# Writing GpSimd's indexed fetches of a four-layer graph network out tile by tile

## The reference

```
x = x + L0(relu(layernorm(x)))   # 4-head attention: q[src]*k[dst], softmax over each dst, sum of v[src], gate, layernorm
x = x + L1(relu(layernorm(x)))   # edge weight = sigmoid(mlp(x[src], x[dst])), symmetric degree norm, sum of (x W)[src]
x = x + L2(relu(layernorm(x)))   # two graph convolutions in a row, each a normed sum of (x W)[src] over dst
x = x + L3(relu(layernorm(x)))   # 4-head graph attention: leaky(e_l[src]+e_r[dst])+log(w), softmax, sum of (x W)[src]
```

## Time and profile before

| | us |
|---|---|
| median of three runs | 8741.41 |
| lowest and highest | 8729.65, 8745.29 |
| span of the profiled execution | 8272.4 |

### The profile page before, as it was taken

One profiled execution on the slowest core, in us unless ns is written; L12 is line 12 of the kernel. 1 busy time (PEld: TensorE's weight loads), 2 busy tenths in 40 slices (PEclk: granted clock), 3 DMA queues, 4 the chain that ended last, 5 costly groups with the idle time before them and its releaser, 6 DMA issues. The chain is left out here.

```text
span 8272.4 us, 99941 instructions
## 1 busy us (share of the span) xinstructions
PE 3960.1 (48%) x22250; PEld 3653.4 (44%) x22250; DVE 3397.9 (41%) x8039; ACT 2027.6 (25%) x3881; POOL 4970.2 (60%) x5007
## 2 busy tenths in 40 slices
PE   4444442553666665666333333433333545454166
PEld 3444441552666665566333333433333444444155
DVE  4333336776444444776322222322222311111586
ACT  1000000773333333996000000000000200000176
POOL 3777772541777775332577777477777277777254
PEclk8555555986666666877656555755555655555599
DMA  5666662441555554663111111111111244444154
GB/s 159 183 180 182 182 182 81 142 121 47 136 134 133 135 137 125 193 196 123 42 47 47 47 47 46 42 47 47 47 47 48 48 96 99 99 99 96 42 155 120
DMA packets 973113, 863.79 MB, mean 104 GB/s; under 512 B 350004, under 2 KB 837256, under 8 KB 972808
## 3 DMA queue, kind: packets, MB, share of 16 engines
q1 hardware_dynamic: 798344, 452.32, 19.6%
q0 software_dynamic: 159744, 356.39, 16.9%
q10 hardware_dynamic: 14976, 54.53, 2.0%
HBM read 669.20 MB, written 193.56 MB: 104 GB/s over the span
## 5 line engine op out<-in xcount | busy, mean ns | idle before, releaser
L768 POOL DMA_INDIRECT sum_rows<-tab_row,sum_idx x1664 | 1644.5, 988 | 631.5 <-issue 470.9
L905 DVE TENSOR_TENSOR acc<-acc,sum_pA 128x128 f32 x4160 | 984.8, 288 | 1846.0 <-PE sum_pA L802 1766.4
L391 PE MATMUL l_pK<-l_winr,l_hotT 128*128 128x128 f32 (+2 forms) x4992 | 1128.0, 399 | 1044.1 <-ACT l_hotT L433 396.2
L391 PEld LDWEIGHTS l_pK<-l_winr,l_hotT 128*128 128x128 f32 x4992 | 1075.7, 327 | 1139.9 <-issue 600.0
L802 PE MATMUL sum_pA<-sum_hot,sum_rows 128*128 128x128 f32 x3328 | 772.8, 426 | 1596.7 <-DMA sum_rows<-tab_row,sum_idx 1596.7
L802 PEld LDWEIGHTS sum_pA<-sum_hot,sum_rows 128*128 128x128 f32 x3328 | 719.7, 328 | 1649.7 <-DMA sum_rows<-tab_row,sum_idx 867.7
L373 POOL DMA_INDIRECT l_rows<-tab_ax,l_idx x832 | 878.1, 1055 | 316.4 <-issue 235.4
L373 POOL DMA_INDIRECT l_rows<-tab_qv,l_idx x832 | 861.9, 1036 | 316.4 <-issue 220.8
L373 POOL DMA_INDIRECT l_rows<-tab_wh,l_idx x832 | 808.2, 971 | 316.3 <-issue 230.9
L802 PE MATMUL sum_pA<-sum_hot,sum_wrow 128*128 128x128 f32 x4992 | 738.8, 310 | 416.5 <-DVE sum_hot L261 233.2
L802 PEld LDWEIGHTS sum_pA<-sum_hot,sum_wrow 128*128 128x128 f32 x4992 | 679.1, 219 | 464.7 <-POOL sum_wrow L737 272.4
(11 more groups left out here) (233 smaller groups left out, 4482.7 us busy)
## 6 DMA issues: line engine op xcount, KB each, us to landing
spill<-l_rows SPq DMA_DIRECT2D x312, 512.0 KB, 3.4
sum_rows<-spill SPq DMA_DIRECT2D x312, 512.0 KB
l_winr<-tab_k SPq DMA_DIRECT2D x840, 64.0 KB
sum_line<-src_lo ACTq DMA_DIRECT2D x104, 512.0 KB, 4.5
l_winr<-tab_b SPq DMA_DIRECT2D x840, 32.0 KB
sum_rows<-tab_row,sum_idx POOLq DMA_INDIRECT x1664
l_winr<-tab_er SPq DMA_DIRECT2D x840, 2.0 KB
l_rows<-tab_qv,l_idx POOLq DMA_INDIRECT x832
```

Of the source, the lines that this page charges most:

```text
L391: last = nc.tensor.matmul(pK[:, b, u, :], hotT[:, b, u, :], winr[:, b * TB + u, :], start=True, stop=True)
L768: nc.gpsimd.indirect_dma_start(rows[:, u, :], None, tab_row, bass.IndirectOffsetOnAxis(idx[:, u:u + 1], 0)).then_inc(s_rows[b], 16)
L905: nc.vector.tensor_tensor(acc[:, u % 2, bass.ds(at, P)], acc[:, u % 2, bass.ds(at, P)], pA[:, b, u, :], ALU.add).then_inc(s_add, 1)
```

## The change

In both functions GpSimd's hardware loop is replaced by a Python loop over all 104 batches, so the 832 indirect DMAs of a phase stand in the code one after the other, and each reads its indices from its own column of `src_idx`. The tile `idx`, the copy, the semaphore `s_idx` and its two waits are gone. The waits for a free half and for the spill keep their counts, now constants. The loops of all other engines stay.

```diff
-                        with pool.Fori(0, ROUNDS) as i:
-                            for b in range(2):
-                                pool.wait_ge(s_used, i * 2 + b + 1)
-                                pool.wait_ge(s_spill[b], i * 16 + 16)
-                                nc.gpsimd.tensor_copy(idx[:, b * TB:(b + 1) * TB],
-                                                      src_idx[:, bass.ds((i * 2 + b) * TB, TB)]).then_inc(s_idx, 1)
-                                pool.wait_ge(s_idx, 1)
-                                pool.wait_ge(s_idx, i * 2 + b + 1)
-                                for u in range(b * TB, (b + 1) * TB):
-                                    nc.gpsimd.indirect_dma_start(
-                                        rows[:, u, :], None, table,
-                                        bass.IndirectOffsetOnAxis(idx[:, u:u + 1], 0)).then_inc(s_rows[b], 16)
+                        for n in range(BATCHES):
+                            b = n % 2
+                            pool.wait_ge(s_used, n + 1)
+                            pool.wait_ge(s_spill[b], 16 * (n // 2) + 16)
+                            for u in range(TB):
+                                t = n * TB + u
+                                nc.gpsimd.indirect_dma_start(
+                                    rows[:, b * TB + u, :], None, table,
+                                    bass.IndirectOffsetOnAxis(src_idx[:, t:t + 1], 0)).then_inc(s_rows[b], 16)
```

23 lines of the change are left out of this document (8 added, 15 removed).

## The result

| | before | after |
|---|---|---|
| median (20 runs each, in turns), us | 8744.34 | 8763.37 |
| lowest, highest | 8727.09, 8770.09 | 8741.39, 8783.59 |
| profiled execution, own time | not given | 8780.58 |
| its span | 8272.4 | 8778.8 |

After over before is 1.0018, with a 95% interval of 1.001 to 1.0025. The change makes the kernel 19 us slower, and the forecast was 377 us less.

What follows compares the result with a forecast made beforehand. GpSimd's own stream was taken to bound the five fetch phases. Boundaries save 352 us and collisions 25, together 377, so 8741.4 falls to 8364 us; the forecast's own range is 8320 to 8412, with two rivals 8250 to 8520.

Steps and rivals of the forecast that it cites:

- The removed part: GpSimd's batch boundaries in five phases: without copy, semaphore and loop, gaps fall from 0.975 to 0.305 us, 352 us saved.
- The collisions: GpSimd fetches starting under VectorE instructions with two SBUF inputs: cost falls from 244 to 219 us, a gain of 25.
- the replay: Last 103 batches of each phase recomputed with fetches at their new places: 17, 59, 34, 36 and 73 us of collisions.
- The rule of 0.82: A fetch starting under a VectorE instruction with two SBUF inputs ends no earlier than 0.82 us behind that instruction.
- all on the path, since GpSimd waits for nobody: All five phases last as long as GpSimd's own stream, so the whole 352 us saved at boundaries shortens the kernel.
- over 4 us of cover: Used rows, needed free about 10.2 us behind a batch's last fetch, are free by about 5.6 to 5.8 us.
- I keep the 469 as it is: The runs' median lies 469 us above the profiled span; this unexplained part was taken to stay constant.
- One of the prediction's own signs of being wrong: Idle of GpSimd before fetches put down to VectorE, TensorE or the spill would show the forecast wrong.
- GpSimd's pace being set by something unseen: Rival: the change doesn't do what it says and the time stays the same; chance 0.03.
- The score passes are held by transfers: Rival: SyncE's windows or the DMA engines become the bound, only the sums gain, 133 us: 8608 us; chance 0.04.
- the second rival: More is gained: collisions vanish with small shifts, or the 469 us is a stretch; 8250 to 8315 us, chance 0.08.
- The slower rival: GpSimd's 4160 unrolled fetches wait for instruction blocks; at 10 us for each of 49 blocks 8854 us; chance 0.07.

Runs made afterwards that it cites:

- x_before: The kernel before, run and recorded again unchanged; 8649.83 us, 1.0017 of the kernel before.
- a_pace_score: The changed kernel with a 1,024-column memset and a wait for it ahead of each batch in the three score passes only; 8453.32 us, 0.9788 of the kernel before.
- a_fetchonly: The changed kernel with sums 2 and 3 reduced to their fetches, VectorE running a free loop in sum 3; 8788.39 us, 1.0175 of the kernel before.
- a_fo_rate: The changed kernel, both sums only fetches with VectorE's free loop, rests of 1,024 columns (sum 2) and 1,536 (sum 3); 8814.24 us against 8654.08 for before.
- a_pace1024: The changed kernel with a 1,024-column memset and a wait for it ahead of each batch, in all phases; 8503.15 us, 0.9879 of the kernel before.
- a_pace2048: The changed kernel with a 2,048-column memset and a wait for it ahead of each batch, a rest of 2.09 us; 8756.58 us, 1.013 of the kernel before.
- a_half: The changed kernel with each fetch of the two plain sums cut from 128 to 64 rows, the others zeros; 8700.0 us, 1.01 of the kernel before.

## Why the prediction was wrong

**The removed part was right.** The gap at a boundary is 0.305, the fetch's median 0.944 to 0.946 (0.947 to 0.949 before), and GpSimd's first fetch starts at 117.9, 2.2 us earlier. If the stops are taken out, GpSimd's own stream (busy time, gaps inside batches, 0.305 at 103 boundaries) is 1083, 1100, 1109, 1115 and 1093 us, together 5500. The forecast's five phases sum to 5504.

**The collisions were right in sum.** They cost 29, 52, 64, 69 and 43 us (busy time less 832 medians), 257 where the replay had 219. The sums have more and score 3 less than forecast; the replay knew of no stops, and these shift the fetches against VectorE. The rule of 0.82 held: the fetch of 4567.82 starts under the one-hot that ends at 4568.31 and ends at 4569.13.

```profile
4566.57 0.94 POOL L756 DMA_INDIRECT sum_rows<-tab_row,src_idx  x1 [0.30 <-issue]
4567.09 1.22 DVE L261 TENSOR_TENSOR sum_hot<-iota,local 128x1024 f32<-128x1024 f32 x1
4567.82 1.31 POOL L756 DMA_INDIRECT sum_rows<-tab_row,src_idx  x1 [0.30 <-issue]
```

The one-hot starts inside the fetch of 4566.57, which keeps its 0.94. So this trace differs again from the Trainium skill, "SBUF — State Buffer", section "SBUF: two separate sides", by which the first of the two holds the port pair for its whole instruction.

**The step that failed is "all on the path, since GpSimd waits for nobody", with its "over 4 us of cover".** The phases took 6394 us and not 5504: 890 us of stops, 713 of them in the score passes and 179 in the sums. The cover was computed with VectorE's and SyncE's instructions at the speed that they had in the recording. That speed didn't hold: single register instructions took 0.70 or 1.40 us, eight window loads 12.74 us for 4.00, and what TensorE signals came up to 9.6 us late in the sums. So the spill goes out late and a half of `rows` is free late, and GpSimd stops. This is what the profile shows. In sum 2 the prediction had TensorE done 5.8 us behind the last fetch, read off a first add that followed the matmuls by 0.24 us. Why all this is late is the theories' part. D, taken from fetches alone, puts the limit at 8 x 1.40 = 11.2 us a batch; in the whole sums slow instructions remain at 11.7 us a batch and are gone at 12.3, so there it lies higher. The kernel before, with 11.01 to 11.68 us (the phases of its first recording over 104), stood near such a limit by the accident of its copy and its wait. The forecast's 10.3 to 10.9 us a batch (1074 to 1130 over 104) is below it, by D 0.3 to 0.9 us of lag in each batch. The sums then settle at 11.5 whatever the gap (1194 to 1203 us in the seven kernels with gaps of 0.3 to 0.8 whose sums fetch all their rows). In the score passes the stops are longer than what was saved (12.6 to 13 us a batch in score 0, 11.65 in x_before).

**"I keep the 469 as it is" failed too.** It was the trace's one warning, a span and a time that didn't fit, and I carried it along as a constant. In x_before GpSimd's own stream is 5854 us and its stops 350; in the recording its stops are nil. The cost that would grow was already in the timed runs, and only there. One of the prediction's own signs of being wrong is what came: idle time of GpSimd before fetches put down to VectorE or the spill.

**The rivals.** "GpSimd's pace being set by something unseen" had 0.03 and is what happened. "The score passes are held by transfers, SyncE's windows the bound, and only the sums gain" named the right engine, with transfers and not slow issues as the reason, and gave the sums a gain that they didn't have. (The sum for the range takes the second rival at 0.07; it stands in the list at 0.08.) The slower rival, code passed once, isn't borne out: the instruction queue took 64 packets for 30, and the gaps inside batches sum to 228 to 236 us a phase for 235 before, which leaves no time for late blocks. This agrees with what the Trainium skill, "Runtime: NRT & Kernel Launch", section "Instruction fetch mechanics", says of straight code.

**What stays open.** What it is that is worked off at 1.40 us a fetch, and why it stretches register instructions of two engines and delays what a third, TensorE, signals. It may be the recording itself, whose lost records come with the slow instructions; no unrecorded time is at hand to tell. Whether the pace or the length of the rest decides, since the whole sums still have slow instructions at 1.46 us a fetch with rests of 1.24. Why the first recording had none of it, though its sums ran at 11.1 to 11.17 us a batch, just under 11.2. And why SyncE is slow in the score passes after 4 to 10 fetches and at paces above 1.40 (158 stretched ones in a_pace_score's score 3 at 11.86 us a batch): SyncE's own DMAs may count too, which wasn't tried.

## What to carry to other kernels

When the recorded span and the timed runs differ by far more than the runs do among themselves, the recording shows another execution than the one to be improved; take a second one before any sum is made, and count what each holds: one with a third of its semaphore steps can't be trusted for what ended a wait. An engine that "waits for nobody" may still be kept in step by its own small delays: before removing them, ask what rate they hold it to and what shares that rate. For a stream of indexed fetches on GpSimd, try a short rest for each batch and measure it phase by phase; here a rest of 1.24 us per eight fetches in the passes where SyncE issues nine DMAs a batch took 2.1% off the time, and the same rest in the two sums as well gave only 1.2%.

## What the runs showed of the hardware

All of this holds for recorded executions.

- Unbroken indirect DMAs of 128 rows on GpSimd go at 1.25 us each for some 200 of them and then at 1.40 (0.947 and 1.095 us, with 0.305 between them; a_fetchonly).
- In a phase of fetches alone with a rest after each eighth, nearly all register instructions of VectorE take 0.70 us after about 60 fetches at a mean pace of 1.366 us and rests of 1.24; at 1.42 us and rests of 1.66 none does (a_fo_rate). After unbroken fetches this lasts some 27 us beyond the last one (a_fetchonly). In the whole sums some still do at 1.46 us and rests of 1.24 (a_pace1024), and none at 1.53 and 2.09 (a_pace2048).
- In the same executions what TensorE signals reaches VectorE and GpSimd up to 9.6 us behind the recorded end of the matmul, for 0.24 us in the first recording (the changed kernel, kernel before).
- A fetch of 64 rows takes 0.903 us, one of 128 rows 0.944, and both have the same number of DMA packets and much the same effect on VectorE's instructions (263 and 229 of over 0.4 us; a_half and the changed kernel).
